# A graph-attention kernel on one core: one gather in twenty groups moves from GpSimd to single-row transfers issued by SyncE

## The chip, the cores and the metric

One Trainium2 chip, one of its cores. The metric is the device time of one execution in microseconds, lower is better. The kernel before takes 2794.09 us (median of three runs, 2792.91 to 2798.66).

## What is computed

Two layers of graph attention over 3125 nodes of 128 features, with 103125 edges (50000 drawn pairs in both directions and 3125 self loops; the network adds another self loop per node). Cut to what matters:

```python
for l in range(2):
    xn = layernorm(x)
    xp = xn + xn @ Wpos + degree term
    q, k, v = xp @ Wq, xp @ Wk, xp @ Wv              # 8 heads of 16
    att = clip(einsum('ehd,ehd->eh', q[dst], k[src]) / 4, -50, 50)
    ex = exp(att - segment_max(att, dst)[dst])
    aggr = segment_sum(v[src] * ex / segment_sum(ex, dst)[dst], dst)
    x = x + aggr @ Wo
    x = x + gelu(layernorm(x) @ W1) @ W2
```

The edges are sorted by destination. What costs time is to fetch the row `k[src], v[src]` (256 floats, 1 KB) for every edge and to sum over edges by destination.

## The kernel before

The edges stand in 806 tiles of 128 edges. Four tiles make a group; a layer has 202 groups (the last one has two tiles), the two layers 404. Groups 0 to 5 of a layer (the seam groups) hold the tiles in which one block of destinations ends and the next begins.

Each layer writes its keys and values to a table in HBM, `kv_table[l]`. **GpSimd** then gathers for each group one tile after the other, 128 rows of 1 KB per indirect DMA, into `kvr`, a ring of eight groups (`RING`, line 801). Before group n it waits for `s_msg`, that is until VectorE has used the values of group n-8. **ScalarE** makes the one-hot matrix of the destinations from `relT` (lines 1279 and 1283) and the exponentials (1289, 1292). **TensorE** spreads the queries over the edges (line 1079) and sums the messages by destination (line 1092). **VectorE** multiplies keys and queries (`prod`, line 1675), reduces, clips, multiplies values by weights (`msg`, line 1697), adds the sums of the group before last to `agg` (line 1706, four or five times) and builds the other one-hot matrix (line 1667). Each engine has its own program; the order inside it is written out by hand, slot by slot: slot s of a layer is group s, and the dense work of a chunk of two or three blocks (output projection, layer norms, feed-forward, the next layer's q, k, v) is placed at fixed distances behind the group that ends the chunk.

**SyncE** computes nothing. It issues the loads, and later, also slot by slot: `rel_rows(body)` (lines 634 and 637), a broadcast of the next four one-hot tiles' numbers from `rel_table` to all partitions, 512 KB, into one of two halves of `relT`, as soon as ScalarE has done with that half; `load_x0` (679); `load_loops(c)` in layer 0 (672), `store_table` for the next layer (688), `store_out` in the last (697). Several of these take a register for the number of a block, which a TENSOR_LOAD reads from SBUF first.

At the start SyncE waits for `rankT`, stores `rankrow`, loads biases, writes `rel_table`, issues the first two `rel_rows`, writes the first table, and then moves the 25 blocks of q and the 25 of x to their ranks (655, 660). Then the loop over the slots begins. The steps of the prediction touch `rel_rows`, the loop over slots on SyncE, GpSimd's loop over groups (line 801), `edge_spread` on ScalarE, and `edge_prod` and `edge_msg` on VectorE.

Of the kernel before, what the change touches and what calls it, by code (L numbers as in the profile page):

```python
# [25 lines left out]
I32 = mybir.dt.int32  # L26
# [7 lines left out]
P = 128  # L34
N, D, H, L, FF = 3125, 128, 8, 2, 512
HD = D // H
# [119 lines left out]

def step_of(n):

    return n // GROUPS, n % GROUPS


def gathers(n):

    return min(G, TILES - n % GROUPS * G)

# [35 lines left out]
def landed(n):  # L201

    return 16 * sum(gathers(k) for k in range(n % RING, n + 1, RING))
# [67 lines left out]
def build(nc, x_in, src_flat, src_tiles, dst_tiles, dst_last, weights, out):  # L271
    with ExitStack() as ctx:
# [56 lines left out]
        kvr = sb("kvr", [P, RING, G, KV])  # L329
        onehot = sb("onehot", [P, OH, G, P])  # L330
# [173 lines left out]
        s_kv = [sem(f"s_kv{r}") for r in range(RING)]  # L504
        s_oh = sem("s_oh")
# [96 lines left out]
        def _(sp):  # L602
# [10 lines left out]
            sp.wait_ge(s_blockrank, 1)  # L613
            sp.wait_ge(*read(0, 0, "rankT"))
# [10 lines left out]
            def rel_rows(body):  # L625

                if body >= 2:
                    sp.wait_ge(s_ohT, (body - 1) * BODY)
                group = group_of(body * BODY)
                to = relT[:, body % 2, :, :].rearrange("p r c -> p (r c)")  # L630
                if is_seam(group):
                    ends = row_of(group) - ROW_END
                    rows_of = rel_table[ROW_END:ROW_END + 2 * (ROW_BEGIN - ROW_END), :].rearrange("(a h s) e -> a h s e", a=1, h=2)
                    sp.dma_start(to.rearrange("p (h c) -> p h c", h=2),
                                 rows_of[:, :, ends:ends + 2 * G, :].rearrange("a h s e -> a h (s e)").broadcast_to([P, 2, 2 * G * P])).then_inc(s_relT[body % 2], 16)
                else:
                    sp.dma_start(to, rel_table[row_of(group):row_of(group) + BODY * G, :].rearrange("(a s) e -> a (s e)", a=1).broadcast_to([P, BODY * G * P])).then_inc(s_relT[body % 2], 16)
# [62 lines left out]

            for l in range(L):
# [16 lines left out]
        def _(pool):  # L718
# [70 lines left out]
            for n in range(L * GROUPS):  # L789
# [9 lines left out]
                for j in range(gathers(n)):  # L799
# [313 lines left out]
        def _(act):  # L1113
# [156 lines left out]

            def edge_spread(n):

                for h, m in enumerate(hots(n)):
# [9 lines left out]
                    act.activation(onehotT[:, m % OHT, :, :].rearrange("p j e -> p (j e)"), apart[:], ACT.Relu, bias=1.0, scale=-1.0).then_inc(s_ohT, 1)  # L1283

# [25 lines left out]
        def _(dve):  # L1310
# [359 lines left out]
            def edge_prod(n):  # L1670
# [3 lines left out]
                t = gathers(n)  # L1674
                dve.tensor_tensor(prod[:, 0:t, :], kvr[:, n % RING, 0:t, 0:D], bank[2][:, 0:t * D].rearrange("p (j c) -> p j c", c=D), ALU.mult).then_inc(s_prod, 1)  # L1675
# [17 lines left out]
            def edge_msg(n):  # L1693

                dve.wait_ge(s_ex, n + 1)
                t = gathers(n)
                dve.tensor_tensor(by_head(msg[:, n % 2, 0:t, 0:D]), by_head(kvr[:, n % RING, 0:t, D:KV]),  # L1697
                                  ex[:, 0:t * H].rearrange("p (j h) -> p j h", h=H).unsqueeze(3).broadcast_to([P, t, H, HD]), ALU.mult).then_inc(s_msg, 1)
# [127 lines left out]
```

## Time and profile before

| | |
|---|---|
| median of three runs | 2794.09 us |
| profiled execution, from its first to its last instruction | 2183.8 us |
| what lies outside that span, against the median | 610.3 us |
| GpSimd busy | 1570.6 us (72%) |
| VectorE busy | 1710.2 us (78%) |
| TensorE matmul busy | 1419.8 us (65%) |
| ScalarE busy | 940.2 us (43%) |
| mean busy share of the 16 DMA engines | about 45% |

The profiled execution's own time is its span; the profile shows nothing of what lies outside. Busy does not count the gap that GpSimd leaves between two indirect DMAs, nor anything on SyncE, whose instructions are all of the kind that issues DMAs or loads registers. They are seen in the timeline under the name SPq. Where a table of waits names "issue", the profile shows nothing that the engine waited for.

### The profile page before, as it was taken

Reading aid. Unit: us, or ns where it says so; the run is one execution under the profiler, and the core shown is the slowest. Engines: PE = TensorE matmul, PEld = TensorE weight load, DVE = VectorE, ACT = ScalarE, POOL = GpSimd, SP = SyncE. Lnnn points to the kernel's source line nnn. Section 1 sums busy time; section 2 is a strip of 40 time slices with the busy share of each in tenths; the row PEclk is TensorE's granted clock in tenths of the full one; section 3 lists DMA queues with packets and bytes.
Section 4 is the critical chain, followed back from the end, with each engine's and each line's share of the span. In section 5 each row is a group of like instructions: output and inputs, shape, how many; then the busy total and the mean of one; then the engine's idle time right before and its main releaser. Section 6 shows DMA issues by size and latency. Waiting matters only on the chain.

```text
span 2183.8 us, 32409 instructions
## 1 busy us (share of the span) xinstructions
PE 1419.8 (65%) x8227; PEld 1237.3 (57%) x8227; DVE 1710.2 (78%) x5103; ACT 940.2 (43%) x2179; POOL 1570.6 (72%) x1669
## 2 busy tenths in 40 slices
PE   4866576666667676766666657566666757666666
PEld 4555565656555565655556556556555656555555
DVE  8759888888877878787877777777777778777775
ACT  8334353534535353534454335343343435343344
POOL 6277777777777777777727777777777777777773
PEclk9979888877878788887988787787787778787787
DMA  2365445444444444444424444444444444444441
GB/s 87 119 178 182 148 133 154 147 136 134 142 134 125 142 134 142 124 142 134 132 69 143 135 125 136 137 123 139 133 139 124 139 134 129 134 134 138 125 138 56
DMA packets 123505, 289.29 MB, mean 132 GB/s; under 512 B 31525, under 2 KB 57057, under 8 KB 123329
## 3 DMA queue, kind: packets, MB, share of 16 engines
q0 software_dynamic: 77824, 212.31, 33.8%
q1 hardware_dynamic: 45504, 74.92, 10.3%
q8 instruction: 76, 1.25, 0.2%
q14 instruction: 101, 0.82, 0.1%
HBM read 275.44 MB, written 8.38 MB: 130 GB/s over the span
## 4 chain that ended last, share of the span: by engine, by line
POOL 47%; issue 20%; DVE 11%; PE 11%; DMA 6%; ACT 3%; DVEq 1%; SPq 0%; ACTq 0%
POOL kvr L801 47%; DMA kvr<-kv_table,srcidx 5%; PE bank L1079 4%; PE bank L1092 3%; DVE agg L1706 3%; DVE kvr L1322 2%; DVE prod L1675 1%; DVE msg L1697 1%; ACT apart L1279 1%; ACT onehotT L1283 1%; DVE onehot L1667 1%; PE bank L1036 1%; PE bank L1015 1%; PE bank L816 1%; PE bank L894 1%
## 5 line engine op out<-in xcount | busy, mean ns | idle before, releaser
L801 POOL DMA_INDIRECT kvr<-kv_table,srcidx x1612 | 1530.7, 950 | 547.4 <-issue 480.0
L1079 PE MATMUL bank<-q,onehotT 128*128 x3320 | 606.8, 340 | 712.1 <-DVE prod L1675 475.2
L1079 PEld LDWEIGHTS bank<-q,onehotT 128*128 128x128 f32 x3320 | 515.6, 237 | 825.5 <-issue 824.8
L1092 PE MATMUL bank<-msg,onehot 128*128 128x136 f32 x3320 | 612.3, 344 | 1.9 <-DVE msg L1697 1.9
L1289 ACT ACTIVATE bank<-attc 128x32 f32<-128x32 f32 x404 | 81.2, 201 | 1145.7 <-DVE attc L1691 1145.0
L1092 PEld LDWEIGHTS bank<-msg,onehot 128*128 128x128 f32 x3320 | 571.8, 252 | 3.6 <-DVE msg L1697 3.3
L1675 DVE TENSOR_TENSOR prod<-kvr,bank 128x512 f32<-128x512 f32 x404 | 276.0, 683 | 302.6 <-DMA kvr<-kv_table,srcidx 264.0
L1706 DVE TENSOR_TENSOR agg<-agg,bank 128x136 f32 x1624 | 469.1, 289 | 44.9 <-PE bank L1092 40.1
L1279 ACT ACTIVATE apart<-relT,minus_p 128x512 bf16<-128x512 bf16 x416 | 293.8, 706 | 4.4 <-DMA relT<-rel_table 4.0
L1667 DVE TENSOR_TENSOR onehot<-bank,rel 128x512 f32<-128x512 f32 x416 | 282.5, 682 | 0.2
L1697 DVE TENSOR_TENSOR msg<-kvr,bank 128x512 f32<-128x512 f32 x404 | 273.9, 678 | 5.0 <-ACT bank L1289 4.9
L1680 DVE TENSOR_REDUCE att<-prod 128x32 f32<-128x512 f32 x404 | 272.9, 676 | 0.1
L1283 ACT ACTIVATE onehotT<-apart 128x512 f32<-128x512 bf16 x416 | 261.9, 629 | 13.1
L1292 ACT ACTIVATE msg<-attc 128x32 f32<-128x32 f32 x404 | 85.9, 213 | 0.0
L1686 DVE TENSOR_SCALAR attc<-att 128x32 f32<-128x32 f32 x404 | 78.3, 194 | 0.0
L1691 DVE COPY_PREDICATED attc<-attnan,zeros 128x32 f32<-128x32 uint8 x404 | 77.0, 191 | 0.0
L1685 DVE TENSOR_TENSOR attnan<-att 128x32 uint8<-128x32 f32 x404 | 74.0, 183 | 0.1
L1548 DVE TENSOR_TENSOR x<-x,bank 128x384 f32<-128x384 f32 (+1 forms) x36 | 18.9, 524 | 62.9 <-PE bank L1036 33.7
L1289 ACT ACT_TABLE_LOAD x51 | 65.4, 1283 | 0.9
L1036 PE MATMUL bank<-w,hT 128*128 128x128 f32 x400 | 59.8, 294 | 0.0
L1322 DVE TENSOR_TENSOR kvr<-kvr,q 128x3328 bf16<-128x3328 bf16 (+1 forms) x32 | 55.0, 1770 | 2.2 <-PE bank L828 2.1
L1023 PE MATMUL bank<-xnT,w 128*128 128x384 f32 (+1 forms) x144 | 56.3, 523 | 0.7 <-ACT xnT L1216 0.7
(217 smaller groups left out, 844.5 us busy)
## 6 DMA issues: line engine op xcount, KB each, us to landing
relT<-rel_table SPq DMA_DIRECT2D x104, 512.0 KB, 4.1
kvr<-kv_table,srcidx POOLq DMA_INDIRECT x1612
loop_kv<-kv_table SPq DMA_DIRECT2D x25, 128.0 KB, 3.9
kv_table<-qkv SPq DMA_DIRECT2D x25, 128.0 KB, 3.2
kv_table<-onehot SPq DMA_DIRECT2D x8, 256.0 KB, 2.2
w<-weights SPq DMA_DIRECT2D x2, 840.0 KB, 7.4
loops<-x_in SPq DMA_DIRECT2D x5, 320.0 KB, 5.6
q<-qkv SPq DMA_DIRECT2D x25, 64.0 KB
```

The source lines that it names most:

```text
L801: pool.indirect_dma_start(kvr[:, n % RING, j, :], None, kv_table[l], bass.IndirectOffsetOnAxis(ap=srcidx[:, step:step + 1], axis=0)).then_ ...
L1079: mm = pe.matmul(bank[2][:, j * D:(j + 1) * D], onehotT[:, m % OHT, j, :], q[:, bass.ds(ranks[j + h], 1), :].rearrange("p a c -> p (a c)") ...
L1092: mm = pe.matmul(sum_ps(n, k), onehot[:, m % OH, j, :], msg[:, n % 2, j, :], start=(m, j) == of[0], stop=(m, j) == of[-1])
L1279: act.activation(apart[:], relT[:, m // BODY % 2, r, :], ACT.Abs, bias=minus_p[:]).then_inc(s_apart, 1)
L1283: act.activation(onehotT[:, m % OHT, :, :].rearrange("p j e -> p (j e)"), apart[:], ACT.Relu, bias=1.0, scale=-1.0).then_inc(s_ohT, 1)
L1289: act.activation(ex[:, 0:t * H], attc[:, n % 2, 0:t * H], ACT.Exp).then_inc(s_ex, 1)
L1322: return dve.tensor_tensor(oh[:, k % 2, :, :, :], digit[:, 0:count_of, :].unsqueeze(1).broadcast_to(shape), of_step.unsqueeze(2).broadcast ...
L1667: dve.tensor_tensor(onehot[:, m % OH, :, :], iota_ps.unsqueeze(1).broadcast_to([P, G, P]), rel[:, row:row + G].unsqueeze(2).broadcast_to([ ...
L1675: dve.tensor_tensor(prod[:, 0:t, :], kvr[:, n % RING, 0:t, 0:D], bank[2][:, 0:t * D].rearrange("p (j c) -> p j c", c=D), ALU.mult).then_in ...
L1680: dve.tensor_reduce(att[:, n % 2, 0:t * H], prod[:, 0:t, :].rearrange("p j (h d) -> p (j h) d", d=HD), AX, ALU.add).then_inc(s_att, 1)
L1697: dve.tensor_tensor(by_head(msg[:, n % 2, 0:t, 0:D]), by_head(kvr[:, n % RING, 0:t, D:KV]), ex[:, 0:t * H].rearrange("p (j h) -> p j h", h ...
L1706: dve.tensor_tensor(target, target, sum_ps(n, j), ALU.add).then_inc(s_agg, 1)
```

## The change

In each layer ten groups are named: 33, 49, 65 and so on to 177. Of each, GpSimd gathers three tiles instead of four. The fourth tile is fetched by SyncE, one DMA of 1 KB per row, 128 per tile, into one of two buffers `row_kv`. SyncE issues sixteen rows at every second slot from slot 12 on, so eight slots' steps make a tile, and the last sixteen rows of a tile stand seven slots ahead of the group that uses them. The sixteen row numbers are read by a register load from `row_src`, ten rows of SBUF filled at the start by ten small DMAs. Before a tile SyncE waits until VectorE has used the tile before last. VectorE's `prod` and `msg` become two instructions each in these groups, the first over three tiles, the second over the one from `row_kv`. All `rel_rows` from the third on are issued by ScalarE, right behind the activation that leaves the half of `relT` free.

```diff
+ROW_FROM, ROW_EVERY, ROW_CHUNK, ROW_MARGIN = 12, 2, 16, 5
+ROW_CHUNKS = P // ROW_CHUNK
+ROW_TILES = 10
+ROW_GROUPS = [ROW_FROM + (i + 1) * ROW_CHUNKS * ROW_EVERY + ROW_MARGIN for i in range(ROW_TILES)]
+ROW_BUFS = 2
+def pooled(n):
+    return gathers(n) - by_rows(n)
...
@@ SyncE, at the start @@
+            sp.wait_ge(s_rows, 16 * 2 * SC)
+            for i, g in enumerate(ROW_GROUPS):
+                c, p = divmod(row_of(g) + G - 1, P)
+                sp.dma_start(row_src[i:i + 1, :], step_src[p:p + 1, c * P:(c + 1) * P]).then_inc(s_row_src, 16)
             sp.wait_ge(*read(0, 0, "rankT"))
...
-                if body >= 2:
-                    sp.wait_ge(s_ohT, (body - 1) * BODY)
...
+            sp.wait_ge(s_row_src, 16 * ROW_TILES)
             for c, (b0, nb) in enumerate(NAT):
...
+            def fetch_rows(l, k):
+                i, part = divmod(k, ROW_CHUNKS)
+                tile = l * ROW_TILES + i
+                if part == 0:
+                    if k == 0 and l:
+                        for u in range(2):
+                            c = NCH - 1 - u
+                            sp.wait_ge(s_table[buffer(l, c)], stored(l, c))
+                    if tile >= ROW_BUFS:
+                        back = tile - ROW_BUFS
+                        sp.wait_ge(s_msg, back // ROW_TILES * GROUPS + ROW_GROUPS[back % ROW_TILES] + 1)
+                e0 = part * ROW_CHUNK
+                rows = nc.values_load_multi_w_load_instructions(row_src[i:i + 1, e0:e0 + ROW_CHUNK], ...)[1]
+                for j, r in enumerate(rows):
+                    sp.dma_start(row_kv[e0 + j:e0 + j + 1, tile % ROW_BUFS, :], kv_table[l][bass.ds(r, 1), :]).then_inc(s_row_kv[tile], 16)
@@ SyncE, the loop over slots @@
-                    for body in range(2, L * BODIES):
-                        if s < GROUPS and group_of((body - 1) * BODY - 1) - 1 == l * GROUPS + s:
-                            rel_rows(body)
+                    k, off = divmod(s - ROW_FROM, ROW_EVERY)
+                    if off == 0 and 0 <= k < ROW_TILES * ROW_CHUNKS:
+                        fetch_rows(l, k)
@@ GpSimd @@
-                for j in range(gathers(n)):
+                for j in range(pooled(n)):
@@ ScalarE, edge_spread @@
+                    if m >= BODY and m % BODY == 0 and m // BODY + 1 < L * BODIES:
+                        rel_rows(m // BODY + 1)
@@ VectorE, edge_prod; edge_msg likewise @@
-                t = gathers(n)
+                t = pooled(n)
...
+                if by_rows(n):
+                    dve.wait_ge(s_row_kv[row_tile(n)], 16 * P)
+                    ins = dve.tensor_tensor(prod[:, t, :], row_kv[:, row_tile(n) % ROW_BUFS, 0:D], bank[2][:, t * D:(t + 1) * D], ALU.mult)
```

## Rows read from the trace of the kernel before

**Rows 1.** Page: share of the chain that ended last, by engine, by line.

```profile
POOL 47%; issue 20%; DVE 11%; PE 11%; DMA 6%; ACT 3%; DVEq 1%; SPq 0%; ACTq 0%
```

**Rows 2.** Waits: engine, line, waited for: us in total, times, longest; whole span.

```profile
POOL kvr L801 <- issue: 480.0, 1575, 0.3
...
POOL kvr L801 <- DVE msg L1697: 11.2, 35, 0.8
```

**Rows 3.** Timeline of GpSimd: start, duration, what, idle before; three stretches of 1612.

```profile
97.82 0.99 POOL L801 DMA_INDIRECT kvr<-kv_table,srcidx  x1 [21.51 <-DMA kv_table<-xn]
...
171.02 0.95 POOL L801 DMA_INDIRECT kvr<-kv_table,srcidx  x1 [0.30 <-issue]
...
184.80 0.95 POOL L801 DMA_INDIRECT kvr<-kv_table,srcidx  x1 [0.31 <-issue]
...
1108.54 0.95 POOL L801 DMA_INDIRECT kvr<-kv_table,srcidx  x1 [0.30 <-issue]
1144.17 0.95 POOL L801 DMA_INDIRECT kvr<-kv_table,srcidx  x1 [34.69 <-DMA kv_table<-qkv]
...
2153.47 0.94 POOL L801 DMA_INDIRECT kvr<-kv_table,srcidx  x1 [0.30 <-issue]
```

**Rows 4.** Groups by shape: op, count, busy and mean ns, idle before, releasers.

```profile
L1675 DVE TENSOR_TENSOR prod<-kvr,bank 128x512 f32<-128x512 f32 x402 | 275.2, 684 | 302.3 <-DMA kvr<-kv_table,srcidx 264.0 <-PE bank L1079 16.0 <-issue 8.6
L1706 DVE TENSOR_TENSOR agg<-agg,bank 128x136 f32 x1624 | 469.1, 289 | 44.9 <-PE bank L1092 40.1 <-DVE agg L1706 1.1 <-issue 0.6
L1542 DVE TENSOR_TENSOR xn<-agg,rsum 128x384 f32<-128x384 f32 x14 | 7.8, 558 | 0.5
```

**Rows 5.** Waits in the stretch 184 to 1109 us, layer 0 behind its start.

```profile
DVE prod L1675 <- DMA kvr<-kv_table,srcidx: 76.0, 58, 4.1
```

**Rows 6.** Timeline of VectorE: group 33 of layer 0, group 177 of both layers.

```profile
272.00 0.69 DVE L1675 TENSOR_TENSOR prod<-kvr,bank 128x512 f32<-128x512 f32 x1 [1.08 <-DMA kvr<-kv_table,srcidx]
...
994.66 0.69 DVE L1675 TENSOR_TENSOR prod<-kvr,bank 128x512 f32<-128x512 f32 x1 [2.85 <-DMA kvr<-kv_table,srcidx]
...
2039.00 0.69 DVE L1675 TENSOR_TENSOR prod<-kvr,bank 128x512 f32<-128x512 f32 x1 [1.73 <-DMA kvr<-kv_table,srcidx]
```

**Rows 7.** Timeline of SyncE's queue: start, length of the run, what, count.

```profile
66.86 0.94 SPq L615 DMA_DIRECT2D rankrow<-rankT  x1
...
118.19 18.19 SPq L660 DMA_DIRECT2D x<-x_nat  x25
...
170.69 14.01 SPq L679 DMA_DIRECT2D x_nat<-x_in  x25
...
201.28 1.40 SPq L672 DMA_DIRECT2D loop_kv<-kv_table  x3
```

**Rows 8.** Single lines: durations min/median/max in ns, first and last start.

```profile
L672 SPq DMA_DIRECT2D loop_kv<-kv_table x25: 332/342/355, 201.3 to 472.3; - x25
...
L596 SPq TENSOR_LOAD <-permrow x27: 275/669/674, 200.4 to 2168.9; - x27
```

**Rows 9.** Waits of SyncE's own queue: the start's longest.

```profile
SPq L614 <- DVE rankT L1462: 59.5, 1, 59.5
```

**Rows 10.** Single line: the gathers of the row numbers at the start.

```profile
L753 POOL DMA_INDIRECT q<-src_tiles,tileno x7: 945/1492/1565, 27.2 to 37.3; - x7
```

**Rows 11.** Stretch: length, PE, PEld, DVE, ACT, POOL busy, clock, DMA share, GB/s.

```profile
171.00:185.00 14.00, 10.06 (x58) 9.03 (x56) 12.46 (x39) 5.55 (x15) 10.63 (x12) 0.76 0.82 249
```

**Rows 12.** Waits of ScalarE; page's group of line 1279.

```profile
ACT bank L1289 <- DVE attc L1691: 1145.0, 358, 11.9
...
L1279 ACT ACTIVATE apart<-relT,minus_p 128x512 bf16<-128x512 bf16 x416 | 293.8, 706 | 4.4 <-DMA relT<-rel_table 4.0
```

**Rows 13.** Single line: what the other relT issues take on SyncE.

```profile
L637 SPq DMA_DIRECT2D relT<-rel_table x98: 319/320/472, 137.1 to 2114.1; - x98
```

**Rows 14.** Page: span; DMA queue, kind: packets, MB, share of 16 engines.

```profile
span 2183.8 us, 32409 instructions
...
q8 instruction: 76, 1.25, 0.2%
```

More of the change, by code:

```diff
@@ L164, in gathers, with by_rows, row_tile @@
     return min(G, TILES - n % GROUPS * G)
+def by_rows(n):
+    return n % GROUPS in ROW_GROUPS
+def row_tile(n):
+    l, g = step_of(n)
+    return l * ROW_TILES + ROW_GROUPS.index(g)
+def pooled(n):
+    return gathers(n) - by_rows(n)
 def is_seam(n):
@@ L201, in landed @@
 def landed(n):
-    return 16 * sum(gathers(k) for k in range(n % RING, n + 1, RING))
+    return 16 * sum(pooled(k) for k in range(n % RING, n + 1, RING))
 def blocks_by(c):
@@ L329, in build @@
         kvr = sb("kvr", [P, RING, G, KV])
+        row_kv = sb("row_kv", [P, ROW_BUFS, KV])
+        row_src = sb("row_src", [ROW_TILES, P], I32)
         onehot = sb("onehot", [P, OH, G, P])
@@ L504, in build @@
         s_kv = [sem(f"s_kv{r}") for r in range(RING)]
+        s_row_src = sem("s_row_src")
+        s_row_kv = [sem(f"s_row_kv{i}") for i in range(L * ROW_TILES)]
         s_oh = sem("s_oh")
@@ L699, in store_out @@
                     sp.dma_start(out[RANKED * P:N, :], x[0:TAIL, RANKED, :]).then_inc(s_out, 16)
+            def fetch_rows(l, k):
[10 more added lines that the diff above has]
+                e0 = part * ROW_CHUNK
+                rows = nc.values_load_multi_w_load_instructions(row_src[i:i + 1, e0:e0 + ROW_CHUNK], engines=(ENG.SP,), min_val=0, max_val=NP - 1,
+                                                                skip_runtime_bounds_check_because="sources are numbers of nodes")[1]
+                for j, r in enumerate(rows):
+                    sp.dma_start(row_kv[e0 + j:e0 + j + 1, tile % ROW_BUFS, :], kv_table[l][bass.ds(r, 1), :]).then_inc(s_row_kv[tile], 16)
             for l in range(L):
                 for s in range(SLOTS):
-                    for body in range(2, L * BODIES):
-                        if s < GROUPS and group_of((body - 1) * BODY - 1) - 1 == l * GROUPS + s:
-                            rel_rows(body)
                     if (l, s) == (0, 2 * BODY):
                         load_x0()
+                    k, off = divmod(s - ROW_FROM, ROW_EVERY)
+                    if off == 0 and 0 <= k < ROW_TILES * ROW_CHUNKS:
+                        fetch_rows(l, k)
                     for c, at in parts_at(s, LATE_SP):
@@ L1269, in dense_parts, with rel_rows @@
                             loop_exp(phase, c)
+            def rel_rows(body):
+                act.wait_ge(s_ohT, (body - 1) * BODY)
+                group = group_of(body * BODY)
+                to = relT[:, body % 2, :, :].rearrange("p r c -> p (r c)")
+                if is_seam(group):
+                    ends = row_of(group) - ROW_END
+                    rows_of = rel_table[ROW_END:ROW_END + 2 * (ROW_BEGIN - ROW_END), :].rearrange("(a h s) e -> a h s e", a=1, h=2)
+                    act.dma_start(to.rearrange("p (h c) -> p h c", h=2),
+                                  rows_of[:, :, ends:ends + 2 * G, :].rearrange("a h s e -> a h (s e)").broadcast_to([P, 2, 2 * G * P])).then_inc(s_relT[body % 2], 16)
+                else:
+                    act.dma_start(to, rel_table[row_of(group):row_of(group) + BODY * G, :].rearrange("(a s) e -> a (s e)", a=1).broadcast_to([P, BODY * G * P])).then_inc(s_relT[body % 2], 16)
             def edge_spread(n):
@@ L1695, in edge_msg @@
                 dve.wait_ge(s_ex, n + 1)
-                t = gathers(n)
-                dve.tensor_tensor(by_head(msg[:, n % 2, 0:t, 0:D]), by_head(kvr[:, n % RING, 0:t, D:KV]),
-                                  ex[:, 0:t * H].rearrange("p (j h) -> p j h", h=H).unsqueeze(3).broadcast_to([P, t, H, HD]), ALU.mult).then_inc(s_msg, 1)
+                t = pooled(n)
+                ins = dve.tensor_tensor(by_head(msg[:, n % 2, 0:t, 0:D]), by_head(kvr[:, n % RING, 0:t, D:KV]),
+                                        ex[:, 0:t * H].rearrange("p (j h) -> p j h", h=H).unsqueeze(3).broadcast_to([P, t, H, HD]), ALU.mult)
+                if by_rows(n):
+                    ins = dve.tensor_tensor(msg[:, n % 2, t, 0:D].rearrange("p (h d) -> p h d", d=HD), row_kv[:, row_tile(n) % ROW_BUFS, D:KV].rearrange("p (h d) -> p h d", d=HD),
+                                            ex[:, t * H:(t + 1) * H].unsqueeze(2).broadcast_to([P, H, HD]), ALU.mult)
+                ins.then_inc(s_msg, 1)
             def edge_add(n, j, ranks):
```

3 lines of the change are left out of this document (2 added, 1 removed).

## The prediction

> **What bounds the kernel now.** I read the chain that ended last first: GpSimd's gathers hold 47% of it, and the 20% named issue are mostly the gaps between them [rows 1]. The waits of GpSimd say the same from the other side. It waited 21.5 us for the first layer's table and 34.7 us for the second's [rows 3], but only 11.2 us in 35 short stops for VectorE to free a slot of the ring; the other 480.0 us before its gathers are the 0.3 us after each one [rows 2]. So from the first gather of a layer to its last GpSimd never stops. The timeline gives its pace: layer 0 runs from 97.82 to 1108.54 us in 805 steps, 1.2555 us each; layer 1 from 1144.17 to 2153.47, 1.2538 us [rows 3]. A group of four costs 5.02 us. VectorE has the larger busy share, 78%, yet it stands 302 us idle ahead of `prod`, 264.0 of it for a gather to land [rows 4]. It is the second bound, with about 0.7 us of room in a group, less in layer 0 (76.0 us between 184 and 1109 us [rows 5]) than in layer 1.
>
> **What GpSimd saves.** Ten gathers in each layer go, 20 of 1612. As GpSimd paces both layers, each takes one step off its end: 10 x 1.2555 + 10 x 1.2538 = 25.1 us. A layer's tail (the last groups on VectorE, the last chunks, the table, 35 us between the layers) hangs on the last gathers and moves with them. The dropped time must also be used by VectorE. Between two named groups lie sixteen groups; VectorE idles there for gathers on average 16 x 76.0/185 = 6.6 us in layer 0 (185 groups at 5.02 us are the stretch), and GpSimd's lead grows by only 1.25 us. Even a stretch with half that room absorbs it, so I take all of it; the bounds are 25.1 us and, if layer 0 gave nothing, 12.5 us.
>
> **VectorE's extra instructions.** A named group has 384 + 128 columns where it had 512, twice. A 384-wide instruction took 558 ns, a 136-wide one 289 ns, the 512-wide one 684 ns [rows 4]: 163 ns more, 0.33 us in a group, 6.5 us in all. It lies in the 302 us of idle time before `prod`, and in these groups GpSimd is 1.25 us early anyway. I cost it at nothing; with the cover gone it is 6.5 us. The new wait on `s_row_kv` stands ahead of the second half of `prod`; behind it queue all adds, `msg` and the one-hot of later groups, so a late tile stops VectorE and through the ring, eight groups later, GpSimd.
>
> **SyncE's start.** The ten copies of row numbers wait for the gathers of line 753, the last of which starts at 37.3 us [rows 10]. SyncE now waits 59.5 us for `rankT` and goes on at 66.86 us [rows 9, 7]. The nearest copy between rows of SBUF, `rankrow`, takes 0.94 us [rows 7], so ten take some 9 to 10 us from about 40 us, done by 50, hidden in that wait. If the row numbers came 20 us later, they would delay `rankrow` by some us: bound 0 to 5, I take 0.
>
> **SyncE's rows.** This is the large unknown: 2560 DMAs with a register as the row of the table. The trace has no single-row DMA from HBM. The nearest row is `loop_kv`, also out of `kv_table` with a register on the HBM side: its instruction takes 342 ns, and three in 1.40 us make (1.40 - 0.34)/2 = 0.53 us from start to start [rows 7, 8]. The other ends are `load_x0`, 25 in 14.01 us with seven register loads, which leaves 0.475 between two, and `x` to its ranks, 25 in 18.19 us, which is 0.64 to 0.73 with both ends in SBUF [rows 7]. I take 0.53, since source and register are the same. Sixteen rows are then 8.5 us and one TENSOR_LOAD of 0.28 to 0.67 us [rows 8], 9.1 us against two slots of 5.02. A tile takes SyncE 128 x 0.53 + 8 x 0.67 = 73 us. In layer 0 nine visits each of `load_loops` and `store_table` at about 2.1 us (a load of 0.67 and 1.4 for three blocks) are 3.8 us more per tile, 77 us in all, against 80.3 us for sixteen groups. It fits by 4%.
>
> **When the rows must be there.** `rel_rows`, where SyncE waited for ScalarE, no longer holds it back, so `load_x0` follows the 25 blocks of x at 136.4 us instead of 170.7 [rows 7], and the first row goes out at about 153 (14.0 us for those loads and some 2.5 for the last block of x to land). Ten tiles at 77 us end at 923. Group 177 uses the tenth, at 994.66 - 11.3 = 983 us [rows 6]; less 4 us to land that is 979, 56 us of room. Group 33 wants the first at 272 us [rows 6], and it is there by about 235. In layer 1 there are no loops and the rows begin behind the table at 1144. There 1147 + 10 x (128 x 0.53 + 6.7) = 1892 stands against 2039.00 - 24 - 4 = 2011 [rows 6] (6.7 us are the loads of the row numbers and 1.3 for the stores of the output), the wider room of the two. So the rows cost nothing in the likeliest case.
>
> **The relT loads on ScalarE.** 102 DMA issues of 320 ns (what they take on SyncE [rows 13]), 33 us, are now in ScalarE's program behind an activation. What follows is the exponential of the next group, for which ScalarE waited 1145.0 us in 358 of 404 cases, 3.2 us each [rows 12]. Hidden there; in the other 46 cases it may delay something, 33 x 46/404 = 3.8 us at most. The load has four groups to land. One gain: the third `rel_rows` no longer queues behind the blocks of x until 136.4 us, which cost ScalarE part of 4.0 us [rows 7, 12]; but GpSimd hardly stops then, so 0 to 0.5 us. Net I take 0.
>
> **Traffic.** The rows add no bytes: what SyncE fetches, GpSimd doesn't. What could matter is the pace of the gathers: 15.8 ns more on each of 1592 would eat the 25.1 us. In the stretch 171 to 185 us, with 25 block loads of SyncE in flight and the DMA engines at 0.82 [rows 11], the gathers kept (184.80 - 171.02)/11 = 1.2527 us [rows 3], no more than the mean of a layer. I take 0; bounds -2 to +5 us.
>
> **Sum.** The profiled span is 2183.8 us, so 2183.8 - 25.1 = 2158.7. The 610.3 us up to the median lie outside it and I carry them over: 2794.1 - 25.1 = 2769.0 us.
>
> **A rule that speaks against it.** The Trainium skill, DMA: Bandwidth & Descriptors, Rules for kernel authors, says of many small transfers that they should be merged, since below 64 KB one pays mostly overhead, and it puts the fixed cost of a DMA at about 2.0 us. If SyncE paid those 2.0 us for each row one after the other (an estimate by that page), a tile would take 256 us instead of 73 and the kernel would be far slower. The trace speaks against that reading: SyncE starts a block every 0.475 to 0.73 us [rows 7] while each takes some 4 us to land. The overhead that remains is the issue time, and that is the first rival.
>
> **Rivals.**
> A. *SyncE is too slow with the rows* (slower than before). Ten tiles fit layer 0 while 153 + 10 x (128p + 9.2) <= 979, that is up to p = 0.573 us per row; 0.53 is 8% below. Beyond it VectorE waits for rows and both layers stretch. At p = 0.60 layer 0 ends 34 us later, layer 1 still fits: net +9, 2803 us. At 0.64, the shortest step of x to its ranks, layer 0 loses 85 and layer 1 23: 2877 us. For it: single rows are not in the trace, and copies with both ends in SBUF take this much. Against: both transfers that read HBM are at 0.475 to 0.53. Chance 0.11.
> B. *VectorE uses only part* (it is nearly full in stretches of layer 0, its extra instructions and ScalarE's issues show): 12.5 us from layer 1 and little from layer 0, 2775 to 2786. Against: 6.6 us of idle per sixteen groups. Chance 0.08.
> C. *The gain is eaten by traffic or by a longer part outside the span*. SyncE's program grows by some 8000 instructions (three per row, as at line 672) on 32409 [rows 14]; the profile can't show what this does outside its span. It would end near 2794, between 2788 and 2800. Against: instructions are fetched inside the span, 1.25 MB by one queue with 0.2% of the engines' time [rows 14]. Chance 0.06.
> The forecast has 0.75.
>
> **How the numbers follow.** A change of 0.2%, 5.6 us, is about what a measurement of this kernel can tell from none. Forecast and B are faster, 0.83. C is within it, 0.06. A is slower, 0.11. The forecast's own range is 2764 to 2775. The whole range reaches over B and C to the first case of A, 2762 to 2803, and leaves out most of A.
>
> **What would show it.** GpSimd's gathers: 1592 at 1.252 to 1.256 us, its waits for `msg` still near 11 us. SyncE: rows 0.5 to 0.53 us apart, waiting for `msg` at the tiles' heads. VectorE: no wait for `row_kv`, and 1.25 us more idle before `prod` nowhere needed. ScalarE: waits for `relT` gone. Wrong would be: rows 0.58 us apart or more, or VectorE idle before the second `prod` of a named group.

## The result, and the profile after

The changed kernel takes 2972.85 us (median of four runs, 2969.82 to 2974.01) against 2793.52 us (2792.91 to 2798.66): ratio 1.0625, 95% interval 1.0602 to 1.0649, 179 us slower. I had said 25 us faster, with 2803 us as the upper end of the range.

The page of the changed kernel, its span, busy times and the chain that ended last (shares by engine, then by line; compare [rows 1]):

```profile
span 2972.3 us, 40280 instructions
...
PE 1693.0 (57%) x8227; PEld 1477.4 (50%) x8227; DVE 1714.0 (58%) x5143; ACT 941.0 (32%) x2179; POOL 1552.5 (52%) x1649
...
SPq 38%; issue 32%; DVE 10%; another core or an unknown queue 10%; PE 7%; ACT 2%; DVEq 1%; DMA 0%; POOL 0%; ACTq 0%
SPq L747 32%; SPq L744 4%; DVE agg L1777 3%; PE bank L1127 3%; PE bank L1140 2%; DVE kvr L1385 2%; DVE onehot L1730 1%; DVE prod L1738 1%; ACT onehotT L1344 1%; PE bank L1084 1%; ACT apart L1340 1%; DVE msg L1764 0%; DVEq L618 0%; PE bank L942 0%
```

GpSimd's 47% of the chain are gone, and SyncE, which had 0%, holds 38% of it: 32% at line 747, the single-row transfers, and 4% at 744, the load of their numbers. The waits of the changed kernel (engine, tile, line, what it waited for: total us, times, longest):

```profile
POOL kvr L849 <- DVE msg L1764: 811.2, 211, 21.6
DVE agg L1777 <- remote: 528.4, 137, 5.6
...
DVE prod L1741 <- DMA row_kv<-kv_table: 166.2, 13, 21.9
```

13 of the 20 tiles came late, and VectorE stood 166.2 us for them. The timeline shows one such stop (start, duration, instruction, in brackets the idle time before):

```profile
1266.13 0.29 DVE L1741 TENSOR_TENSOR prod<-row_kv,bank 128x128 f32<-128x128 f32 x1 [15.46 <-DMA row_kv<-kv_table]
```

Two further lines differ from what I had read. GpSimd, which had waited for `msg` only 11.2 us [rows 2], waits 811.2 us; and the span is 1.7 us below the time of its own execution (2974.01), while before it was 610 us below [rows 14]. The second says that something was wrong with my reading of the kernel before. The first experiment is therefore the kernel before itself. (In these tables "remote" means that the profile found an update of the count that the engine waited for, but no instruction that ended shortly before it.)

### The profile page after: what moved, and what is told of

Same layout as the page of the kernel before. It is cut to its first block, busy times and chain, and to the rows that moved or that the text cites. A ratio compares the mean times of both kernels' runs of the same rounds, so it can differ in the third digit from the quotient of the medians.

```text
span 2972.3 us, 40280 instructions
## 1 busy us (share of the span) xinstructions
PE 1693.0 (57%) x8227; PEld 1477.4 (50%) x8227; DVE 1714.0 (58%) x5143; ACT 941.0 (32%) x2179; POOL 1552.5 (52%) x1649
## 3 DMA queue, kind: packets, MB, share of 16 engines
q8 instruction: 76, 1.25, 0.2%
## 4 chain that ended last, share of the span: by engine, by line
SPq 38%; issue 32%; DVE 10%; another core or an unknown queue 10%; PE 7%; ACT 2%; DVEq 1%; DMA 0%; POOL 0%; ACTq 0%
SPq L747 32%; SPq L744 4%; DVE agg L1777 3%; PE bank L1127 3%; PE bank L1140 2%; DVE kvr L1385 2%; DVE onehot L1730 1%; DVE prod L1738 1%; ACT onehotT L1344 1%; PE bank L1084 1%; ACT apart L1340 1%; DVE msg L1764 0%; DVEq L618 0%; PE bank L942 0%
## 5 line engine op out<-in xcount | busy, mean ns | idle before, releaser
L849 POOL DMA_INDIRECT kvr<-kv_table,srcidx x1592 | 1512.0, 950 | 1329.6 <-DVE msg L1764 811.2
L1127 PE MATMUL bank<-q,onehotT 128*128 x3320 | 707.6, 381 | 864.0 <-DVE prod L1738 316.7
L1127 PEld LDWEIGHTS bank<-q,onehotT 128*128 128x128 f32 x3320 | 615.0, 277 | 975.8 <-issue 973.9
L1140 PE MATMUL bank<-msg,onehot 128*128 128x136 f32 x3320 | 753.7, 399 | 362.1 <-DVE msg L1764 354.2
L1140 PEld LDWEIGHTS bank<-msg,onehot 128*128 128x128 f32 x3320 | 689.7, 297 | 392.1 <-DVE msg L1764 382.8
L1738 DVE TENSOR_TENSOR prod<-kvr,bank 128x512 f32<-128x512 f32 (+1 forms) x404 | 272.8, 675 | 267.2 <-remote 175.1
L1764 DVE TENSOR_TENSOR msg<-kvr,bank 128x512 f32<-128x512 f32 (+1 forms) x404 | 271.3, 671 | 2.8 <-ACT bank L1352 2.8
L1741 DVE TENSOR_TENSOR prod<-row_kv,bank 128x128 f32<-128x128 f32 x20 | 5.7, 285 | 166.2 <-DMA row_kv<-kv_table 166.2
L1753 DVE TENSOR_SCALAR attc<-att 128x32 f32<-128x32 f32 x404 | 88.9, 220 | 0.0
L1084 PE MATMUL bank<-w,hT 128*128 128x128 f32 x400 | 68.4, 317 | 6.9 <-issue 6.8
L1071 PE MATMUL bank<-xnT,w 128*128 128x384 f32 (+1 forms) x144 | 63.6, 579 | 0.7 <-ACT xnT L1264 0.7
```

The costliest lines, as they stand in the source:

```text
L849: pool.indirect_dma_start(kvr[:, n % RING, j, :], None, kv_table[l], bass.IndirectOffsetOnAxis(ap=srcidx[:, step:step + 1], axis=0)).then_ ...
L1127: mm = pe.matmul(bank[2][:, j * D:(j + 1) * D], onehotT[:, m % OHT, j, :], q[:, bass.ds(ranks[j + h], 1), :].rearrange("p a c -> p (a c)") ...
L1140: mm = pe.matmul(sum_ps(n, k), onehot[:, m % OH, j, :], msg[:, n % 2, j, :], start=(m, j) == of[0], stop=(m, j) == of[-1])
L1738: ins = dve.tensor_tensor(prod[:, 0:t, :], kvr[:, n % RING, 0:t, 0:D], bank[2][:, 0:t * D].rearrange("p (j c) -> p j c", c=D), ALU.mult)
L1764: ins = dve.tensor_tensor(by_head(msg[:, n % 2, 0:t, 0:D]), by_head(kvr[:, n % RING, 0:t, D:KV]), ex[:, 0:t * H].rearrange("p (j h) -> p j ...
```

## The experiments

Chips differ: the kernel before takes 2796 (two of them), 2833, 2842 and 2830 us on those used. Only kernels of one chip are compared, each as a ratio to the kernel before on that chip.

**The kernel before once more** (no edit), and **the relT loads alone on ScalarE**, both on one chip with the third kernel below.

> The kernel before, unchanged, to see its own spans: its page had a span of 2183.8 us under a median of 2794 us, while the page of the changed kernel has a span of 2972.3 us under 2974.0 us. Theory S (something outside the kernel's own waits stretches most executions of this program, and the page of before shows one that escaped): the span of this run is within 3 us of its time, near 2790 us. Theory O (610 us of every execution lie outside the span): span 2184 us again.

Measured: 2798.21 us, ratio 1.0006 (0.9994 to 1.0018). Its page and waits:

```profile
span 2797.5 us, 32409 instructions
...
PE 1694.9 (61%) x8227; PEld 1467.7 (52%) x8227; DVE 1711.6 (61%) x5103; ACT 941.3 (34%) x2179; POOL 1567.1 (56%) x1669
...
L801 POOL DMA_INDIRECT kvr<-kv_table,srcidx x1612 | 1526.9, 947 | 1138.2 <-DVE msg L1697 611.7
```
```profile
DVE agg L1706 <- remote: 617.1, 167, 5.8
POOL kvr L801 <- DVE msg L1697: 611.7, 209, 21.5
```

The same program, the same count of instructions, the same busy time of VectorE and GpSimd, but a span of 2797.5 us under a time of 2799.26 us. So the 610 us are inside the span. The execution whose page I had read was no ordinary one: it was over in 2183.8 us. Its granted TensorE clock was 0.810 of full speed, here it is 0.677. In the ordinary execution GpSimd does not run without stops. It waits 611.7 us for `msg`, and VectorE waits 617.1 us before adding to `agg`, for something the table does not name. A gather still takes 0.95 us and the gap 0.30; but they come in bursts, mostly of four or eight. One burst of eight, and TensorE and VectorE beside it:

```profile
1012.00 0.95 POOL L801 DMA_INDIRECT kvr<-kv_table,srcidx  x1 [3.65 <-DVE msg L1697]
...
1013.03 2.02 PE L1092 MATMUL bank<-msg,onehot 128*128 128x136 f32 x8
...
1015.20 0.30 DVE L1706 TENSOR_TENSOR agg<-agg,bank 128x136 f32 x1 [0.73 <-PE bank L1092]
...
1017.53 2.02 PE L1092 MATMUL bank<-msg,onehot 128*128 128x136 f32 x8
...
1020.67 1.15 PE L1079 MATMUL bank<-q,onehotT 128*128 x8 [1.12 <-ACT onehotT L1283]
1020.75 0.95 POOL L801 DMA_INDIRECT kvr<-kv_table,srcidx  x1 [0.30 <-issue]
1023.49 0.29 DVE L1706 TENSOR_TENSOR agg<-agg,bank 128x136 f32 x1 [3.06 <-remote]
...
1024.65 0.94 POOL L801 DMA_INDIRECT kvr<-kv_table,srcidx  x1 [2.96 <-DVE msg L1697]
```

Eight gathers, two groups, in 12.65 us here: 6.3 us a group, where I had 5.02.

These lines also tell what the unnamed wait is. The add at 1015.20 starts 0.15 us after TensorE's sum has ended (1013.03 + 2.02). The sum for the next add ends at 1019.55, TensorE is at its next matmuls at 1020.67, and VectorE, idle from 1020.43, adds only at 1023.49: TensorE's work is done, but VectorE is let go almost 4 us later. Setting each group's sum beside its first add over the whole trace (400 pairs): in 169 of them the add starts over 0.5 us after both the sum has ended and VectorE is free, 556 us in all, and in 166 of the 169 TensorE was by then over 0.5 us into later matmuls. In the page of 2183.8 us there is no such pair, and in the run without gathers below there is none either; the adds that waited for a sum started 0.15 us (median) behind it. So these late starts can account for most of the 613.7 us between the two executions. What holds the message from TensorE back is not shown.

```diff
@@ against the changed kernel @@
 def by_rows(n):
+    return False
-            sp.dma_start(row_src[...], step_src[...])
-                        fetch_rows(l, k)
```

> Only the relT loads move from SyncE to ScalarE; GpSimd gathers all four tiles of every group, no rows are fetched. My sum: no change, 2794 us (2790 to 2798). Rival (the relT issues on ScalarE cost the 178 us): near 2970 us.

Measured: 2798.75 us, ratio 1.0013 (1.0000 to 1.0026). Moving the relT loads costs at most 0.3%, nothing that can be told from zero. That part of the change is out of the question.

**The skipped gathers without the rows.** SyncE fetches nothing, the skipped tile is zeros.

```diff
-                        fetch_rows(l, k)
+            pool.memset(row_kv[:], 0.0).then_inc(s_row_fill, 1)
-                    dve.wait_ge(s_row_kv[row_tile(n)], 16 * P)
+                    dve.wait_ge(s_row_fill, 1)
```

> As the changed kernel, but the 2560 single-row DMAs and their register loads are left out; the tile that GpSimd skips in a named group is zeros, filled once. My sum without the rows: 2794 - 25 = 2769 us. If the skipped gathers save nothing: 2794 us.

Measured: 2749.01 us, ratio 0.9845 (0.9817 to 0.9874), 47 us faster. GpSimd's saving is real and larger than the 25.1 us I gave it. So the loss of 179 us hides a gain of 47; the rows cost some 226 us.

**The rows without their use.** GpSimd gathers all tiles as before, nobody reads `row_kv`; SyncE issues all rows.

```diff
 def pooled(n):
-    return gathers(n) - by_rows(n)
+    return gathers(n)
@@ SyncE, fetch_rows, before a tile @@
+                        sp.wait_ge(s_row_kv[back], 16 * P)
@@ VectorE, twice @@
-                if by_rows(n):
+                if False:
```

> As the changed kernel, but GpSimd gathers all four tiles of every group and VectorE uses those; SyncE issues the same 2560 single-row DMAs at the same slots and is the only one that waits for them. Theory L (the rows come too late: SyncE needs 113 us for a tile, and VectorE's and TensorE's waits on them are the loss): 2795 to 2830 us, a little over before because SyncE's other transfers stand behind the rows. Theory T (the rows' transfers and instructions slow the other engines, whoever waits): 2960 us or more.

Measured: 2882.64 us, ratio 1.0321 (1.0293 to 1.0349), 87 us slower. No compute engine has more instructions and none waits for a row. Issuing rows alone costs more than the skipped gathers give back. A part of it is delay in SyncE's own queue: `loop_kv`, which stands behind the rows there, comes late, and VectorE waits 11.5 us for it, where it did not in the kernel before. What is left of the 179 us is 179 - 87 + 47 = 139 us, next to the 166.2 us that VectorE waited for rows.

**No gathers.** All of the changed kernel but the indirect DMAs of the loop; their tiles are zeros.

```diff
-                for j in range(pooled(n)):
-                    pool.indirect_dma_start(kvr[:, n % RING, j, :], None, kv_table[l], ...)
+                if n == 0:
+                    pool.memset(kvr[:], 0.0).then_inc(s_kvr_fill, 1)
```

> As the changed kernel, but GpSimd gathers nothing: its ring is filled with zeros once, only the ten tiles a layer that SyncE fetches are real. In the changed kernel SyncE's instructions take 0.7 us each while gathers run and a row 0.41 us from start to start while none run. If the gathers are what slows SyncE, all rows here are 0.41 us apart, a tile takes 128 x 0.41 + 8 x 0.7 = 58 us or less, VectorE never waits for rows, and the time falls under 2184 us, to 1800 to 2100 us. If something else slows SyncE (its own number of instructions, or time), its rows keep their mean of 0.85 us.

Measured: 1969.34 us, inside the range expected without late rows. What matters is SyncE: its three instructions per row, by source line (count: shortest/median/longest in ns, first and last start), first without the gathers, then in the changed kernel.

```profile
L748 SPq FUSED_REGOPS  x2560: 37/37/43, 155.1 to 1816.2; - x197
L748 SPq MOVE row_kv<-kv_table x2560: 29/29/39, 155.2 to 1816.2; - x197
L748 SPq DMA_DIRECT2D row_kv<-kv_table x2560: 224/225/496, 155.2 to 1816.3; - x197
```
```profile
L747 SPq FUSED_REGOPS  x2560: 1/37/1395, 190.4 to 2805.5; - x197
L747 SPq MOVE row_kv<-kv_table x2560: 1/29/1398, 190.4 to 2805.6; - x197
L747 SPq DMA_DIRECT2D row_kv<-kv_table x2560: 2/225/1400, 190.5 to 2805.6; - x197
...
L744 SPq TENSOR_LOAD <-row_src x160: 3/1204/1430, 189.3 to 2797.7; - x160
```

The medians are equal and the longest are not: a register move of 29 ns becomes up to 1.4 us. (The load of sixteen numbers takes its 1.2 us with or without gathers, 975/1228/1412 ns in the run without.) When the stretching comes, a part of the changed kernel shows. First a burst of eight gathers, from 406.71 to 416.43 us, with the first add behind it, and a pause from 448.52 to 455.20 us; then SyncE in that burst (7 rows in 8.27 us) and in that pause (14 in 6.18):

```profile
415.48 0.95 POOL L849 DMA_INDIRECT kvr<-kv_table,srcidx  x1 [0.30 <-issue]
...
418.34 0.30 DVE L1777 TENSOR_TENSOR agg<-agg,bank 128x136 f32 x1 [0.89 <-remote]
...
447.57 0.95 POOL L849 DMA_INDIRECT kvr<-kv_table,srcidx  x1 [0.30 <-issue]
455.20 0.95 POOL L849 DMA_INDIRECT kvr<-kv_table,srcidx  x1 [6.68 <-DVE msg L1764]
```
```profile
406.95 8.27 SPq L747 DMA_DIRECT2D row_kv<-kv_table  x7
...
448.70 6.18 SPq L747 DMA_DIRECT2D row_kv<-kv_table  x14
```

In the burst a row takes 1.2 us on average, in the pause about 0.45. Over the whole changed kernel, taking the step between two rows of one sixteen: 1.11 us on average where GpSimd is gathering at the middle of the step (1344 steps), 0.52 where it is not (1056); without gathers at all 0.42, never above 0.79. The mean is 0.848 us, and a tile takes 118 us from its first row to its last. Sixteen groups took 101 to 104 us in the kernel before and 111 in this one, its waits included. It does not fit.

The register instructions are stretched with the DMAs, so it is not the DMA engines' bandwidth alone. The queues of the compute engines are not stretched in the same trace:

```profile
L1777 DVEq FUSED_REGOPS  x1624: 57/57/65, 166.2 to 2954.0; - x181
...
L1330 ACTq DMA_DIRECT2D relT<-rel_table x98: 326/326/339, 171.4 to 2905.6; - x98
```

SyncE's slow stretches and VectorE's late adds end together. In the burst above the last gather ends at 416.43, SyncE is back at 0.41 us a row at 418.1, and VectorE adds at 418.34. Of the changed kernel's 137 late adds, half start 1.7 to 1.9 us after the last gather's end. That both have one cause is likely by this, but not shown.

The shortest times in these lines are a warning: a move that never takes under 29 ns alone is written down with 1 ns. In the ordinary executions the records themselves suffer: of updates of the semaphores (the counts that engines wait for) the trace of 2183.8 us has 38323, the repeat of the same program 15533. Single durations on SyncE are therefore rough. The mean steps and VectorE's waits for the rows do not depend on them. Whether the writing of the records takes part in the stretching, and in what an instruction costs below, no run here tells.

**Fewer tiles.** Seven a layer with sixteen rows every third slot, and five with sixteen every fourth, so that a tile has 24 and 32 groups.

```diff
-ROW_FROM, ROW_EVERY, ROW_CHUNK, ROW_MARGIN = 12, 2, 16, 5
-ROW_TILES = 10
+ROW_FROM, ROW_EVERY, ROW_CHUNK, ROW_MARGIN = 12, 3, 16, 5    # then 12, 4, 16, 5
+ROW_TILES = 7                                                  # then 5
```

> As the changed kernel with seven tiles a layer, 24 groups apart (sixteen rows at every third slot). Theory L: a tile has 24 x 6.8 = 163 us and needs 113, so no wait for rows, and 14 of the 20 skipped gathers' gain stays: 2797 - 14/20 x 47 = 2764 us (2755 to 2785). Theory T: 14/20 of the rows' cost of 223 us as well, 2920 us.

> As the changed kernel with five tiles a layer, 32 groups apart. Theory L: 2797 - 10/20 x 47 = 2773 us (2765 to 2785), no wait for rows. Theory T: 2797 + 10/20 x (223 - 47) = 2885 us.

Measured: 2816.55 us, ratio 1.0083 (1.0053 to 1.0113); and 2808.23 us, 1.0043 (1.0029 to 1.0057). The waits for `row_kv` are gone in both, and most of the loss with them: 179 us become 20.6 and 12.3 by the medians. But it stays a loss, since each tile costs more to issue (87 / 20 = 4.3 us) than its gather gave back (47 / 20 = 2.35 us); by these two, 14 and 10 tiles would lose 27 and 20 us, somewhat more than they did. Giving SyncE time mends the waiting, not the issuing.

**What part of a row costs that?** On another chip (before: 2833.37 us), as the unused rows above, but with row numbers fixed in the program: no TENSOR_LOAD and no register in the address, the same 2560 DMAs.

```diff
-                rows = nc.values_load_multi_w_load_instructions(row_src[...])[1]
-                for j, r in enumerate(rows):
-                    sp.dma_start(row_kv[...], kv_table[l][bass.ds(r, 1), :])
+                for j in range(ROW_CHUNK):
+                    r = (997 * (tile * P + e0 + j)) % N
+                    sp.dma_start(row_kv[...], kv_table[l][r:r + 1, :])
```

> As the run with unused rows (2883 us), but the row of the table is a fixed number: still 2560 DMAs of 1 KB, now one instruction each on SyncE instead of three, and no register loads. If what disturbs the others is the DMAs (data, completions): 2875 to 2890 us again. If it is SyncE's instructions, of which a third is left: 2797 + 87/3 = 2826 us.

Measured: 2863.54 us, ratio 1.0105 (1.0075 to 1.0135), 30 us slower. The DMAs and their bytes are all there, and two thirds of the cost of issuing (87 us, on the other chip) is gone. Beside it a kernel meant to have SyncE's moves and no DMAs:

```diff
+                for j in range(3 * ROW_CHUNK):
+                    sp.reg_mov(spare_reg, j)
```

> As the run with unused rows, but instead of each DMA and its address arithmetic SyncE runs three register moves: 7680 moves and 160 register loads, no row is fetched. If SyncE's instructions disturb the others: 2875 to 2890 us. If the DMAs do: 2795 to 2805 us.

Measured: 2828.28 us, ratio 0.9983 (0.9966 to 1.0000). This run says nothing on its question: the span has 32426 instructions, so the moves had been dropped from the program as having no use. It is the kernel before with the relT loads on ScalarE, and says again that these are free.

**Waiting for the rows, all tiles gathered.** Issue and waiting, without the saving: VectorE waits for `row_kv` before `prod` and then uses GpSimd's tile.

```diff
 def pooled(n):
-    return gathers(n) - by_rows(n)
+    return gathers(n)
@@ VectorE, before prod @@
+                if by_rows(n):
+                    dve.wait_ge(s_row_kv[row_tile(n)], 16 * P)
```

> As the run with unused rows (2883 us), but VectorE waits at each named group until SyncE's tile has landed, without using it; GpSimd gathers all four tiles. The changed kernel is then the sum of skip (-47), issue (+87) and wait (+136 us): here 2797 + 87 + 136 = 3020 us (2990 to 3040). If the wait is not what the rest of the loss is, 2883 us.

Measured: 3067.00 us, ratio 1.0825 (1.0792 to 1.0859), 234 us slower. Its waits:

```profile
DVE prod L1743 <- DMA row_kv<-kv_table: 177.9, 13, 21.1
```

The parts nearly add up: 179 us of the change plus the 47 us of saving that is left out is 226, against 234 on this other chip.

**Forty skipped gathers a layer, no rows.** Is the saving in proportion?

```diff
-ROW_TILES = 10
-ROW_GROUPS = [ROW_FROM + (i + 1) * ROW_CHUNKS * ROW_EVERY + ROW_MARGIN for i in range(ROW_TILES)]
+ROW_TILES = 40
+ROW_GROUPS = list(range(33, 193, 4))
```

> No rows fetched; GpSimd skips one gather in every fourth group, 40 a layer instead of 10 (the skipped tile is zeros). If each skipped gather gives what the ten a layer gave, 47/20 = 2.35 us: 2797 - 188 = 2609 us. If it gives GpSimd's own step of 1.254 us: 2797 - 100 = 2697 us.

Measured: 2733.36 us, ratio 0.9652 (0.9616 to 0.9688), 100 us faster: 1.25 us for each of 80, where 20 gave 2.2 to 2.35 each. Twenty is not a quarter of eighty; why the first ones are worth more stays open.

**All parts on one chip.** The numbers above come from several chips. The four kernels that matter were therefore run on one (before: 2842.46 us): the changed one, rows unused, fixed rows unused, skipping only.

> The changed kernel once more, beside its parts on one chip, since the parts so far were measured on chips on which the kernel before takes 2796 and 2833 us. Expected 1.0625 times before. If the loss is a sum of parts, it equals skip + issue + wait of the runs beside it.

> The 2560 rows with register addresses, used by nobody, beside the fixed rows on one chip. Theory D (the disturbance is the DMAs): the same cost as the fixed rows beside it. Theory I (SyncE's instructions, three a row, and its lateness count too): 1.03 times before as measured, against 1.01 for the fixed rows.

> The 2560 rows at fixed addresses, one instruction each, used by nobody. Theory D: the same as the run beside it with register addresses, near 1.03 on this chip. Theory I: 1.01 times before, a third of the cost beside it.

> 20 gathers skipped, no rows, on the chip of the three others. If a skipped gather gives GpSimd's own step: -25 us. If it gives what it gave the first time: -47 us.

| kernel | us | ratio (95%) | against before |
|---|---|---|---|
| changed | 3060.73 | 1.0764 (1.0746 to 1.0782) | +218.3 |
| rows unused | 2955.39 | 1.0385 (1.0364 to 1.0407) | +112.9 |
| fixed rows unused | 2876.32 | 1.0117 (1.0100 to 1.0134) | +33.9 |
| skipping only | 2798.46 | 0.9853 (0.9824 to 0.9881) | -44.0 |

The same 2560 DMAs cost 113 us with register addresses and 34 without, so theory D, by which they cost the same, fails. And 218 = -44 (gathers skipped) + 113 (rows issued) + 149 (the rest), and in the changed kernel VectorE waits

```profile
DVE prod L1741 <- DMA row_kv<-kv_table: 184.5, 13, 24.0
```

184.5 us for rows. Here both costs are larger than on the first chips (87 and 139), the order is the same. The counts of instructions give a pattern:

```profile
span 2955.3 us, 40279 instructions
```
```profile
span 2878.6 us, 34999 instructions
```

These are rows unused and fixed rows unused, against 32409 before. 7870 more instructions cost 113 us, 14 ns each; 2590 more cost 34 us, 13 ns each (11 and 12 ns on the earlier chips). The first of these is not all the instructions' own: with rows unused VectorE waits 29.3 us for `loop_kv`, which SyncE issues late behind the rows, and with fixed rows not at all.

**Loads instead of DMAs.** If SyncE's instructions cost this whatever they are, then 2560 one-value loads and only 160 DMAs should cost about what the fixed rows did.

```diff
+                rows = [nc.values_load_multi_w_load_instructions(row_src[i:i + 1, e0 + q:e0 + q + 1], ...)[1][0] for q in range(ROW_CHUNK)]
+                total = rows[0]
+                for r in rows[1:]:
+                    total = total + r
+                sp.dma_start(row_kv[e0:e0 + 1, tile % ROW_BUFS, :], kv_table[l][bass.ds(total // ROW_CHUNK, 1), :])
```

> The slots' steps of the changed kernel hold no row DMAs but sixteen register loads of one value each, whose sum is the address of one single 1 KB DMA: 2560 loads and 160 DMAs in place of 160 loads and 2560 DMAs. Nobody uses the result. The fixed rows (2560 instructions that are DMAs) cost 34 us of 2842. Theory D (a DMA's transfer and completion disturb the others): 160/2560 of that, 2 us, same as before within 0.2%. Theory I (any instruction of SyncE does): 34 us or more, 1.012 times before.

Measured: 2859.25 us against 2829.56, ratio 1.0085 (1.0055 to 1.0114), 24 us by the ratio and 30 by the medians. With 3230 more instructions (35639) that is 7 to 9 ns each. It is less than the 34 us that theory I asked for and far from the 2 us of theory D. The DMAs are nearly all gone and the cost is not: it goes rather with what SyncE executes than with what it transfers. It is less per instruction than in the other two, so a count of instructions is a rough measure and no law.

**The changed kernel with fixed rows.** Here the threshold is tried from its other side. With row numbers fixed in the program (they are other rows than the edges name) a tile took 94 us on average, below the 105 to 107 of sixteen groups in those runs. All else is as in the changed kernel, use and waiting included.

```diff
-                for j, r in enumerate(rows):
-                    sp.dma_start(row_kv[...], kv_table[l][bass.ds(r, 1), :])
+                for j in range(ROW_CHUNK):
+                    r = (997 * (tile * P + e0 + j)) % N
+                    sp.dma_start(row_kv[...], kv_table[l][r:r + 1, :])
```

> The changed kernel with all its parts, but each row of the table is a fixed number, so that a row is one instruction on SyncE and a tile takes 94 us instead of 115 (the values are other rows'). If the wait for late rows is a threshold in SyncE's pace (sixteen groups last 108 us), it is gone here: skip -44 and issue +34 leave 0.9965 times before, 2832 us on a chip with 2842. If the loss of the changed kernel has another cause than the pace, it stays near 1.07.

Measured: 2826.35 us against 2829.56, ratio 0.9975 (0.9954 to 0.9995). Its waits name no `row_kv` at all:

```profile
DVE agg L1776 <- remote: 662.9, 153, 5.6
POOL kvr L848 <- DVE msg L1763: 636.7, 200, 25.1
```
```profile
SPq L718 <- DVE qkv L1629: 516.1, 15, 141.6
SPq L727 <- DVE x L1610: 424.1, 6, 131.1
```

The last two lines are SyncE's own waits, ahead of its stores: it now runs so far ahead that it stands for VectorE's results. The mean of 94 us a tile has such stops in it. A tile without one took 51 to 71 us, so the pace is not just under the threshold but far under it.

The sum of the parts is -44 + 34 = -10 us; by the ratio it is -7, by the medians -3. With two instructions less per row and no load, the waiting for rows is gone, and beside it 79 of the 113 us of issuing. It is the only version with rows that is not slower, but it is no kernel, as the row numbers are data.

## Why the prediction was wrong, step by step

**The sum failed first.** "The 610.3 us up to the median lie outside it and I carry them over." They lie inside. I had a page with a span of 2183.8 us under a time of 2794 and took the difference for a constant beside it. In every execution measured afterwards, of whatever kernel, span and time differ by 1.7 to 1.9 us. Every number that I took from the page as a rate (5.02 us a group, 76.0 us of waiting for gathers, GpSimd without stops) belonged to one execution unlike all the timed ones. The carried constant itself did no harm to the sum, as 2797 less 25 is as wrong; the rates did. Where most of the 22% may lie can be told: that execution lacks the 556 us of adds that start late behind finished sums. Why it lacks them is not shown. TensorE's busy time was 1419.8 us there against 1694.9 in the repeat, which is about the ratio of the granted clocks (0.810 and 0.677), but whether a faster TensorE made the execution short or the reverse, no run here tells apart. My rival C came near this place and asked the wrong question, whether the part outside grows.

**What bounds the kernel.** "GpSimd never stops" was right for the page [rows 2] and wrong for the kernel: 611.7 us of waits for `msg`. VectorE's largest wait (617.1 us) is for TensorE's sums, which had mostly been done for microseconds. The rest of the round I argue: a late add holds `msg`, a late `msg` holds the ring, GpSimd stops, and some 1.8 us after it stops the add is let go. With all gathers left out the late adds are gone and the kernel takes 1969 us. No single engine's work is shown to be the bound.

**What GpSimd saves.** Predicted 25.1 us (12.5 to 25.1), measured 44 to 47. The sign was right, the size was not, and the mechanism (GpSimd paces, each gather is one step of 1.2555 us off its end) does not hold in an execution in which GpSimd stands 611.7 us. That forty skipped gathers a layer gave 1.25 us each does not bring it back, as ten gave 2.2 to 2.35.

**SyncE's rows failed second, and this is what made the kernel slower.** The term was 0.53 us a row, from `loop_kv` [rows 7, 8]. As a median it was even too high (0.43), and without gathers the mean is 0.42. The mean is 0.848 us, since SyncE's queue stretches while GpSimd issues gathers. The load of the row numbers, taken as 0.67 us, was 1.2. My rows could not have warned me, because in the execution of that page the stretching is absent: three blocks of `loop_kv` stood 0.53 us apart with gathers running [rows 7]. Rival A was what happened: 13 of 20 tiles late, 166.2 us of waiting, +139 to +149 us. Its threshold of 0.573 us was worked out with 80.3 us for sixteen groups; they took 101 or more, and 0.848 us a row was too slow even for that. I had the place and the mechanism of this part right, gave them 0.11, and my largest price for it, 2877 us at 0.64, was still too low. Fixed rows (no waits) and fewer tiles (no waits) confirm from the other side that it is a matter of SyncE's pace.

**The cost of issuing had no term.** I reckoned SyncE as free as long as it kept up, and for traffic I took 0, bounds -2 to +5. Issuing the rows with nobody to use them cost 87 to 113 us. The bytes are not what costs most: fixed rows move as many in as many DMAs for 30 to 34 us, and loads with hardly a DMA cost 24 to 30. Of the rest 11.5 to 29.3 us are VectorE's waits for `loop_kv`, late behind the rows. How an instruction of SyncE takes 7 to 14 ns from the other engines is not shown. That GpSimd's gathers and SyncE's instructions share something is seen from SyncE's side alone. The Trainium skill, DMA: Bandwidth & Descriptors, Issuing engines are not separate DMA queues, says that the time a sequencer needs to start a DMA is "usually small relative to the DMA itself"; 0.225 us beside the some 4 us of landing that I had used agrees with it. Yet over 2560 of them, with their register moves and stretched, it came to more time than the kernel had.

**The rule that spoke against the change.** The Trainium skill, DMA: Bandwidth & Descriptors, Rules for kernel authors, says to merge small transfers. The price of 2.0 us for each row, paid one after the other, did not come: rows started 0.52 to 1.11 us apart on average. The rule's direction did hold. I had set it aside by the pace alone.

**What was right.** The relT loads on ScalarE cost nothing that shows (1.0013 and 0.9983). SyncE's start was hidden: it still waited 20.4 us for `rankT` in the changed kernel, after 32.0 for the gathered numbers. The extra instructions of VectorE raised its busy time by 2.4 us (1714.0 against 1711.6) and show in no wait.

## What to carry to other kernels

Compare the span of a profile with the time of its run before reading anything else; if they differ by far more than the 1.7 us that is usual here, the page tells of an execution unlike the timed ones, and a second one must be profiled before rates are taken from it. Where a wait has no named releaser, set the producer's end beside the consumer's start: here it told late news from late work. Work moved to an idle queue is not free, and what stands behind it in that queue comes later: cost the issue of each instruction as it runs beside the engines that will be busy then, by the mean and the longest and not by the median, and check first what the bare issue costs, unused. A schedule that fits by 4% on a rate borrowed from another transfer should be treated as one that does not fit.

## What the runs showed of the hardware

- Beside indirect DMAs on GpSimd SyncE's queue stretches in the ordinary executions: register moves from 29 ns to as much as 1.4 us, a row of three instructions from 0.42 us without gathers to 1.11 us on average. Register instructions of VectorE's queue (57 to 65 ns) and DMA issues of ScalarE's (326 to 339 ns) do not stretch in the same trace.
- In the same executions VectorE starts adds up to some 6 us after TensorE's sum has ended (169 of 400 over 0.5 us late, 556 us in all). Without gathers, and in the execution of 2183.8 us, it is 0.15 us.
- An instruction on SyncE whose result nobody uses costs the kernel 7 to 14 ns here.
- A single-row DMA of 1 KB holds SyncE for 0.225 us (median). With a register address and its two register instructions rows are 0.41 us apart (median, without gathers), with a fixed address 0.295 us (median, beside gathers).
- A register load of sixteen numbers from SBUF takes 1.2 us on SyncE, with gathers (1204 ns) and without (1228 ns), one of a single number 0.269 us (medians).
- Of two executions of one program one had a span of 2183.8 us and the other 2797.5 us, with TensorE's mean granted clock at 0.810 and 0.677.
